# Output projection of a fused attention and expert kernel: plain fp32 in place of split fp32r, zero matmuls in front

## What is computed

```python
x = x + xattn(layernorm(x), ctx, Wq, bq, Wk, bk, Wv, bv, Wo, bo)
x = x + ffn(layernorm(x), gate_w, lora_A, lora_B)

# xattn: q = Wq x + bq; k, v from ctx; 8 heads of 16 channels, each query attends to a
# window of 16 keys; then the output projection, which this change is about:
out = softmax(q k / 4) v            # (128 channels, 1024 positions)
return einsum('oc,bct->bot', Wo, out) + bo

# ffn: 8 experts of rank 64 on rows of 1024, the two best by gate, weighted
out += w_full[:, e] * (x @ lora_A[e].T @ lora_B[e].T)
```

## Time and profile before

| | |
|---|---|
| median of 3 runs | 1065.4 us (1064.12 to 1068.92) |
| the profiled execution, its own time | 1065.62 us |
| its span in the trace | 1063.8 us |
| busy share PE / PE loads / DVE / ACT / POOL | 94 / 81 / 82 / 55 / 41% |
| mean granted TensorE clock | 0.987 of full speed |
| instructions | 54664, of them 24452 matmuls and 24452 loads |

### The profile page before, as it was taken

The page is one execution under the profiler, slowest core; times in us unless marked ns, Lnnn a source line. Parts: engine busy times, 40 slices in busy tenths (PEclk is TensorE's granted clock), DMA queues, the critical chain, the costliest instruction groups (busy, mean ns, idle before and its releaser), DMA issues.

```text
span 1063.8 us, 54664 instructions
## 1 busy us (share of the span) xinstructions
PE 1001.7 (94%) x24452; PEld 860.0 (81%) x24452; DVE 873.5 (82%) x1889; ACT 582.5 (55%) x812; POOL 432.3 (41%) x373
## 2 busy tenths in 40 slices
PE   4879999999999999999999999999999999999987
PEld 2768888888888888888887888878888888888866
DVE  3768888889888888888888888888888889898862
ACT  6756555555555555555555554556555555555420
POOL 7774443443343443343434343434443434342210
PEclk9889999999999999999999999999999999999998
DMA  7232333332233332123332223331233332232210
GB/s 269 80 79 85 81 85 101 102 102 67 77 83 83 102 102 81 64 82 83 102 102 64 72 74 99 102 102 47 79 83 103 102 101 58 87 83 63 63 40 40
DMA packets 157721, 92.47 MB, mean 87 GB/s; under 512 B 139728, under 2 KB 139856, under 8 KB 157520
## 3 DMA queue, kind: packets, MB, share of 16 engines
q1 hardware_dynamic: 157520, 89.25, 28.7%
HBM read 55.16 MB, written 16.78 MB: 68 GB/s over the span
## 4 chain that ended last, share of the span: by engine, by line
PE 85%; issue 6%; DVE 5%; ACT 2%; DMA 1%; POOL 1%; DVEq 0%; SPq 0%
PE bank_a L351 34%; PE bank_b L401 17%; PE bank_c L351 16%; PE bank_b L380 13%; PE bank_a L410 5%; DVE stats L811 1%; DMA raw<-x 1%; DVE h_sb L871 0%; DVE row_max L882 0%; DMA prob_t<-ctx 0%; DVE row_sum L896 0%; DVE pick L857 0%; ACT v_sb L652 0%; DVE resid_pair L950 0%; POOL x_split L1116 0%
## 5 line engine op out<-in xcount | busy, mean ns | idle before, releaser
L401 PEld LDWEIGHTS bank_b<-prob_t,v_diag 64*64 64x64 f32 x4608 | 189.5, 134 | 34.9 <-issue 26.4
L351 PE MATMUL bank_a<-down_split,mid_split 128*128 128x264 f32 (+1 forms) x1536 | 213.6, 288 | 1.7 <-issue 1.1
L380 PEld LDWEIGHTS bank_b<-k_sb,q_diag 32*32 32x32 f32 x16384 | 155.7, 104 | 63.8 <-issue 56.5
L401 PE MATMUL bank_b<-prob_t,v_diag 64*64 64x96 f32 (+2 forms) x4608 | 204.7, 239 | 1.0 <-issue 0.9
L380 PE MATMUL bank_b<-k_sb,q_diag 32*32 32x32 f32 x16384 | 173.5, 194 | 29.5 <-issue 25.6
L351 PEld LDWEIGHTS bank_a<-down_split,mid_split 128*128 128x128 f32 x1536 | 193.5, 188 | 8.7 <-issue 2.4
L351 PE MATMUL bank_a<-up_split,ht_split 128*128 128x512 f32 x768 | 195.8, 405 | 3.0 <-DVE ht_split L937 3.0
L1087 POOL TENSOR_TENSOR prob<-prob,row_inv 128x512 f32<-128x512 f32 x128 | 134.2, 1049 | 158.0 <-DVE row_inv L900 156.2
L351 PEld LDWEIGHTS bank_a<-up_split,ht_split 128*128 128x128 f32 x768 | 142.2, 192 | 33.9 <-ACT ht_split L697 3.6
L1110 POOL TENSOR_TENSOR attn_split<-attn,attn_split 128x1024 fp32r<-128x1024 f32 x32 | 76.1, 2380 | 151.5 <-ACT attn_split L672 151.5
L909 DVE STREAM_TRANSPOSE prob_t<-prob 128x768 f32<-128x768 f32 x128 | 123.0, 961 | 0.9 <-POOL prob L1087 0.9
(11 more groups left out here) (77 smaller groups left out, 1303.2 us busy)
## 6 DMA issues: line engine op xcount, KB each, us to landing
v_diag<-v_t SPq DMA_DIRECT2D x128, 132.0 KB, 3.2
raw<-x SPq DMA_DIRECT2D x32, 512.0 KB, 4.8
resid_pair<-x SPq DMA_DIRECT2D x32, 512.0 KB, 4.7
out<-resid_pair SPq DMA_DIRECT2D x32, 512.0 KB, 2.7
raw<-ctx SPq DMA_DIRECT2D x30, 512.0 KB, 3.4
stage<-down_w SPq DMA_DIRECT2D x2, 528.0 KB, 10.6
q_diag<-up_w SPq DMA_DIRECT2D x2, 512.0 KB, 6.0
prob_t<-up_w SPq DMA_DIRECT2D x2, 512.0 KB, 7.5
```

What stands on the lines that cost most here:

```text
L351: return nc.tensor.matmul(dst, st[:, s, st_cols], mv[:, m, mv_cols], start=start and n == 0, stop=stop and n == 2)
L380: last = nc.tensor.matmul(bank_b[m % 2][rows, t * KT:(t + 1) * KT], q_diag[rows, cur.parity, n, :], keys[rows, n * QT:n * QT + KT], start= ...
L401: last = nc.tensor.matmul(bank_b[2 + m % 2][rows, lo * PW:hi * PW], value_blocks(b)[rows, n, :], prob_t[rows, at:at + (hi - lo) * KT], sta ...
```

## The change

`attn_split`, `attention_hi` and `attention_lo` go. The output projection reads `attn` itself and a new tile `wo`, which is loaded once by a DMA of its own (64 KB, issued behind the mask), with two plain fp32 matmuls of 128x512. `even_heads` of chunk 0 now waits for `o_done`. PE starts with 28 plain fp32 matmuls of 128x128 on `prob`, which POOL has set to zero; they write `bank_c`, which nobody reads before the Q projection overwrites it.

```diff
-        attn_split = sb("attn_split", [P, 2, T], F32R)
+        wo = sb("wo", [P, P])
...
                 sp.dma_start(mask[:], mask_in).then_inc(small_in, 16)
+                sp.dma_start(wo[:], wqkvo[:, 3 * P:4 * P]).then_inc(wo_in, 16)
...
             def project_o(b, free):
 
-                pe.wait_ge(attn_hi, b.count(1, 1))
-                pe.wait_ge(attn_lo, b.count(1, 1))
+                pe.wait_ge(attn_done, b.count(CHUNKS, CHUNKS))
+                if first(b):
+                    pe.wait_ge(wo_in, 16)
                 pe.wait_ge(*free)
-                for n in range(6):
-                    last = project_pass(n, bank_c, 3, attn_split)
-                    if n % 3 == 2:
-                        last.then_inc(o_done, 1)
+                for n in range(2):
+                    half = slice(n * HALF, (n + 1) * HALF)
+                    nc.tensor.matmul(bank_c[:, half], wo[:], attn[:, half],
+                                     start=True, stop=True).then_inc(o_done, 1)
+
+            def warm_up(matmuls):
+
+                pe.wait_ge(prob_zero, 1)
+                for n in range(matmuls):
+                    nc.tensor.matmul(bank_c[:, 0:P], prob[:, 0:P], prob[:, 0:P], start=True, stop=True)
 
             def head(b0, b1, b2, b3):
 
+                warm_up(28)
                 first_masks()
...
                 if m == 0 and b.c >= 1:
-                    act.wait_ge(attn_lo, b.count(1, 0))
+                    act.wait_ge(o_done, b.count(2, 0))
...
-            def attention_hi(prev):
...
-            def attention_lo(prev):
```

More of the change, by code:

```diff
@@ L157, in build @@
         bank_c = psum("bank_c", T)
+        wo_in = sem("wo_in")
         small_in, consts_in_sbuf = sem("small_in"), sem("consts_in_sbuf")
@@ L179, in build @@
         exp_done, xt_hi = sem("exp_done"), sem("xt_hi")
-        mask_set, ctx_hi, attn_hi = sem("mask_set"), sem("ctx_hi"), sem("attn_hi")
+        mask_set, ctx_hi = sem("mask_set"), sem("ctx_hi")
         xn_done, xn2_done = sem("xn_done"), sem("xn2_done")
@@ L189, in build @@
         result_done, xt_lo = sem("result_done"), sem("xt_lo")
-        attn_lo, rstd1, xn_lo = sem("attn_lo"), sem("rstd1"), sem("xn_lo")
+        rstd1, xn_lo = sem("rstd1"), sem("xn_lo")
         prob_done, rstd2, ctx_lo = sem("prob_done"), sem("rstd2"), sem("ctx_lo")
@@ L741, in head @@
                 write_mask(b1, 2)
-                attention_hi(b0)
                 exponentials(b1, 3)
@@ L770, in step @@
                     even_heads(prev, 3)
-                    attention_hi(prev)
                 if cur:
@@ L1105, in rows_norm @@
                                         rstd[:, which:which + 1], ALU.mult).then_inc(ready[1], 1)
-            def attention_lo(prev):
-                pool.wait_ge(attn_hi, prev.count(1, 1))
-                nc.gpsimd.tensor_tensor(attn_split[:, 1, :], attn[:], attn_split[:, 0, :].bitcast(F32),
-                                        ALU.subtract).then_inc(attn_lo, 1)
             def normal_lo(later):
@@ L1142, in head @@
                 context_lo(b2)
-                attention_lo(b0)
                 split_lo(7)
@@ L1157, in step @@
                     context_lo(ahead)
-                if prev:
-                    attention_lo(prev)
                 if cur:
```

## The result

The changed kernel takes 1059.39 us (median of 8 runs, 1056.21 to 1061.47), the kernel before beside it 1065.65: a ratio of 0.994, with a 95% interval of 0.992 to 0.996. It is faster, by 0.6%, where 1.5% was forecast; 1059.4 lies within the range, near its slow end. Of all the executions behind this text one is left out, 1584.58 us at a mean granted clock of 0.558 (in the fourth experiment). The profiled execution took 1060.41 us with a span of 1058.6, which is 5.2 less than the span before.

What follows compares the result with a forecast made beforehand. PE's own time was taken as the bound, with issue gaps from fetching 256-instruction blocks. From 1065.62 us: batches -15.1, four further projections +0.8, head +0.2, end -1.5, last step 0, giving 1050 us; 8-in-10 range 1040 to 1061.

Steps and rivals of the forecast that it cites:

- the rival of the lost race: First scores chunk: the packet comes behind data packets, a 0.62 us gap in every batch; 1067 us, no change; chance 0.10.
- the last projection without its wait: End of the run: the last output projection no longer waits 1.56 us for POOL's low part; -1.5 us.
- issue gaps are not fetches: PE's issue gaps keep their sum, only the projection's price is left: +5.1, 1070.7 us; chance 0.06.
- `even_heads` of chunk 0 now waits for the projection ... nothing.: ACT's `even_heads` stands last in its step, so its new wait costs nothing, at most 0.2 us.
- the cover: X normalisation, an exponential and two masks between projection and `even_heads`; without it, at most 0.2 us lost.
- I take +0.2, as DVE's wait is nearest: Head: faster masks and K gain nothing as DVE waits for the second x; loading `wo` first costs +0.2 us.
- I take the low end, since the masks' loads follow at exactly the streaming time.: Output projection: four fp32 records take 1.76 us with edges instead of 1.56, +0.20 us a batch.
- my upper bound of 0.35: Output projection: +0.35 us a batch if each new load shows as in the split product.
- each batch of the changed kernel has the borders of the batch at 930 to 961 us, and I price it by that batch.: 28 batches: standing block borders, 31.00 us each plus 0.20 for the projection, where it was 31.74; -15.1 us.
- Engines relieved ... I cost it at nothing.: ACT and POOL lose an instruction each, DVE's cast falls from 2.23 to some 0.2 us; no gain counted.
- The late batch: The kernel before's batch from 929.89 to 960.89 us, 31.00 us long, its only gap 0.39 us in a weighted chunk.
- my slower rival: Borders up to 56 instructions later, gaps in scores chunks 3 and 1 of every batch: 1091 us; chance 0.04.

Runs made afterwards that it cites:

- the fourth experiment: Changed kernel without zero matmuls in front, with one plain fp32 matmul of 32x32 added ahead of each output projection (1540 instructions a batch): 1067.89 us.
- The two buffers: Changed kernel with two buffers for `attn`, used in turn, so `even_heads` of chunk 0 waits for the projection of the batch before the last: 1055.28 us.

## Why the prediction was right and wrong

**Right: that the gaps are fetches of blocks, and where the borders stand.** 192 packets as before, gaps at one and the same matmul, 3.8 us of them from 420 to 840 us (under 6 was forecast), no gap in chunk 3, none of 0.62 us in chunk 1 (so the rival of the lost race fails), the last projection without its wait (it starts at 1019.98 and lasts 1.88), and that warming buys nothing at the start. The rival "issue gaps are not fetches" is dead: each of the 209 gaps ends 1.2 to 1.6 us after a packet of the queue, and three matmuls on zeros ahead of everything cost 0.9 us, no more than the runs scatter, 28 of them 16.7. With it goes, here, the rule of the Trainium skill ("Runtime: NRT & Kernel Launch", Instruction fetch mechanics) that the fetch hides behind issue: the blocks of 256 agree with the trace, the hiding does not. The advice of the Trainium skill to warm up with matmuls first ("TensorE: Matmul & The Clock Gate", Why this matters for your kernels) is given there for benchmarking a matmul. As to the clock the trace agrees (1.3 us from the masks to K, where it was 2.8); that it would book 3.5 us of a kernel's time was my reading, and no run gained them.

**Wrong, and the largest single item: "`even_heads` of chunk 0 now waits for the projection ... nothing."** I named the cover for the steady batch, where it is there; PE waits for nothing of the kind in the 28. In the head it isn't: the second batch's chunk 0 is done before the first projection. Counted from the first batch's scores chunk 2, since x arrives up to 2 us earlier or later from run to run, the head is 76.50 us before (27.04 to 103.54), 79.77 with the projection alone (26.91 to 106.68), 82.22 with both parts (26.72 to 108.94). The two buffers take back 2.5 to 2.8 us of it, so about 2.7 are the wait, 2.45 the 28 matmuls (issue gaps and the clock), and the remaining 0.6 I haven't traced. The 2.45 answer to the other term that failed in the head, "I take +0.2, as DVE's wait is nearest": it priced the DMA of `wo` and the clock at the start, and not that 28 matmuls shift the borders in the head as well.

**Wrong in size: the projection.** "I take the low end, since the masks' loads follow at exactly the streaming time." At full clock they don't: 1.81 and not 1.76 us, and the transposes ahead of it 0.05 to 0.08 longer; with +0.33 my upper bound of 0.35 was the right end. Against the forecast this is 28 x 0.10 = 3 us, by the table's two rows.

**Wrong in size, because the gap is not fixed by its place: "each batch of the changed kernel has the borders of the batch at 930 to 961 us, and I price it by that batch."** The borders were the same, but one batch was a poor price: its weighted chunk lost 0.39 us, and over 28 batches the loss is 2.00 - 1.51 = 0.49, with waits listed up to 1.0 us. 28 x 0.10 = 3 us. Behind this stands "the fetch takes a fixed time, an estimate of 3 us", counted from where PE enters a block. No row was named for the 3 us; the gaps end 1.7 to 2.9 us after their packet's start. And the start is not fixed to the block: one count less in a wait on ACT moved it by over a microsecond. Nor does "A block of wide matmuls hides the fetch whole" hold everywhere: with 28 matmuls ahead of the split a gap of 1.67 us stood inside a wide product.

**Wrong, though it hid in the sum: "Engines relieved ... I cost it at nothing."** The late batch held no gap in chunk 3, so my sum had this gain in it under another name. But it is not the standing border that brings it: a drifting kernel without the split has no gap in chunk 3 either. Of the 0.72 us there nothing belongs to the borders alone: 0.43 is the wait for `h_sb` that comes with the split, the rest needs the split and a border near. For the same reason my slower rival was mispriced: its place, 14 matmuls on zeros, gave 1063 us and not 1091, and gives 1094 with the split put back.

**The question not asked.** I priced the place of 28 matmuls against the drifting average, and not against the place that the kernel has without them, which was in the same trace: the early batch in the earlier trace rows had no issue gaps. The projection alone is -23 us, and the matmuls on zeros give 16.7 of it back: 28 x 0.50 = 14 in the batches, 2.45 in the head.

## What to carry over

Where dense small matmuls make PE run through a block of 256 instructions in little over a microsecond, count PE's instructions per loop turn (waits too), and try a few harmless instructions more or less ahead: here 3, 14 and 28 of them gave 1044, 1063 and 1059 us. Make the parts of a change separately; two that each look harmless or good can cancel by where they put the rest of the program. And see that the wait ahead of a dense stretch is met early: one count less in a wait on ACT, for gaps on PE, gave 9.7 us.

## What the runs showed of the hardware

- A DVE copy or addition of two numbers a partition lasted 2.05 to 2.12 us on average beside POOL's 128x1024 subtraction, and the copy 0.17 us without it. By the Trainium skill ("SBUF — State Buffer", Terms) DVE and GpSimd share a pair of ports that one of them holds for a whole instruction; the cast, which ends with POOL's subtraction in the earlier trace rows, agrees with that.
- PE can have issue gaps that are decided by when a wait of its stream is met, although its matmuls never stand at that wait: `place_q` was done 0.3 us before the K projection that needs it, the packet started 0.8 us behind that, and the gap came in the next chunk. That the sequencer stands at the wait is inferred.
- A gap inside a group of matmuls ends 1.2 to 1.6 us after the end of the block's packet, in 209 of 209 cases: 519.55 after 518.15 in the version with the split back, 530.34 after 528.90 in the changed kernel, 575.98 after 574.57 in the one with 28 matmuls ahead of the split, and 501.77 after 500.20 in the earlier trace rows.
- The kernel before with 28 matmuls ahead had gaps of up to 2.64 us in scores chunk 2, 1.05 in chunk 0 and 1.67 inside a wide product. Why the fetch is so late at these places stays open.
